# A ring of three score banks for the counts, inverses on 16 columns, and a joined pair of blocks in a decoder layer's attention

## The chip, the cores and the metric

The kernel runs on one core of a Trainium2 chip. The time is that of the device for one execution, in microseconds (us). The engines are TensorE (PE, with its weight loads as PEld), VectorE (DVE), ScalarE (ACT), GpSimd (POOL) and SyncE (SP), which only issues transfers here. All run their own instruction streams and wait for each other by semaphores.

## What is computed

A decoder layer in three parts, each on a layer norm of x and added to it: self-attention with two branches, cross-attention to a memory of 77 rows, and a feed-forward part with weights and activations rounded to FP4. The change touches the self-attention alone, cut to what matters (x is 2 x 2048 x 512, 16 heads of 32):

```python
decay_bias = -jnp.abs(pos[None, :] - pos[:, None]) * (1.0 - decay_factor)
out_short = _attention(q, k_s, v_s, decay_bias)   # softmax(q k^T / sqrt(32) + bias) v
out_long = _attention(q, k_l, v_l, None)
alpha = jax.nn.sigmoid(mix_weight)
out = alpha * out_short + (1.0 - alpha) * out_long
```

## The kernel before, in words

The program has three stages: `project` (projections, to about 480 us), `attend` (to 3794 us), and `finish` (the rest). `attend` treats 32 pairs of batch and head, each with two branches. One branch of one head is a unit, so there are 64 units; a pass of the loop has four (two heads), and `w` is the unit's number in its pass. Even `w` are short branches with the decay, odd ones long branches.

For a unit the scores are made twice. As queries by keys (`scores_qk`, tile `pa`, four PSUM banks), a chunk of 128 queries by 512 keys in a matmul; VectorE takes the row maxima of two chunks at once (`max_pair`). That runs one to two units ahead. The negated maxima are turned, and SyncE writes them as a row of `q_operand` (`place_max`). Then as keys by queries (`scores_kq`, tile `pb`, two banks), with the maxima already subtracted; ScalarE takes the exponential of each chunk of 128 keys by 512 queries into `probs_T`, which has eight slots (`PBUF`) for the 16 blocks of 128 keys.

A unit has 16 steps, one per block. In step `i` TensorE multiplies block `i` with V (`times_v`: four float32 matmuls, each on 32 columns of the array, shown as eight rows), and then issues eight score matmuls: four of `scores_kq` for blocks `i + 1` and `i + 2`, four of `scores_qk` for a later unit. A matmul of `scores_kq` waits for the exponential two chunks before it. In even units a chunk on the diagonal is cut in pieces, with small `kink` matmuls.

The softmax's denominators are sums over all 16 blocks. GpSimd adds ten of the blocks (`BY_POOL`) to `probs_added`, an instruction of 128x2048 each, and issues a DMA for each of the six others (`BY_DMA`), which adds them to `probs_poured` (`pour`; the first one copies). The order of both is `POOL_ORDER`. Each has to wait: an addition for the last one, a transfer for the landing of the last one. ScalarE may write block `b + 8` to the slot of `b` only once V's product, and the addition or the transfer of `b`, are done. Then TensorE sums over the partitions by matmuls with `ones` (`count`, in steps 4 and 6 of the next unit), into a PSUM bank of their own, `pc`.

VectorE's other work in a unit: it copies `outputs_T` from PSUM (`take`, step 15), inverts the sums in four reciprocals of 128x128 (steps 7 to 10), weighs (`weigh`, step 11) and after an odd unit adds both branches (`mix`, step 12). SyncE stores the result, and loads the next operands.

The order on each engine is that in which the loops above write it; nothing schedules it.

## Time and profile before

| what | us |
|---|---|
| median of three runs | 4903.88 (4898.86 to 4909.8) |
| the profiled execution | 4901.64 |
| its span, first to last instruction | 4899.8 |
| TensorE busy | 4676.8 (95%) |
| VectorE busy | 3911.0 (80%) |
| GpSimd busy | 3278.3 (67%) |
| ScalarE busy | 2928.4 (60%) |

The shares are over all stages. A row of PE is one matmul or several alike merged; matmuls are pipelined, so a row is longer than the time to the next one's start, and the time from start to start tells what a matmul costs. In square brackets stands how long the engine was idle before a row, and what ended that.

### The profile page before, as it was taken

How to read it: one execution, taken by the hardware profiler on the slowest of the kernel's cores; microseconds unless marked ns; L12 is line 12 of the kernel's file. 1: busy time of each engine (PE TensorE's matmuls, PEld its weight loads, DVE VectorE, ACT ScalarE, POOL GpSimd, SP SyncE). 2: the span in 40 equal slices, each digit the busy share in tenths (PEclk: the TensorE clock that was granted, in tenths of full speed). 3: DMA queues.
4: the chain of work that ended last, by engine and by line, in shares of the span. 5: the costliest groups of instructions: out<-in, count | busy, mean ns of one | idle time of the engine just before them, and what ended most of it. 6: DMA issues, size and time to landing. Idle time of an engine off the chain costs nothing. (4 is left out here: it accounts for less than half of the span.)

```text
span 4899.8 us, 94453 instructions
## 1 busy us (share of the span) xinstructions
PE 4676.8 (95%) x30732; PEld 2051.3 (42%) x30732; DVE 3911.0 (80%) x4625; ACT 2928.4 (60%) x5106; POOL 3278.3 (67%) x1268
## 2 busy tenths in 40 slices
PE   8998999999999999999999999999998799999998
PEld 3444233333333333333333333333332577777776
DVE  7567888888888888888888888888884588888887
ACT  3222367676766766766666666766666355555554
POOL 0000399998989989888898989989897233333332
PEclk9999799999999999999999999999999799999999
DMA  5444366666676666666666676666765100000000
GB/s 171 126 140 129 84 154 154 152 151 160 146 156 151 157 157 146 159 144 157 153 146 159 144 158 155 157 154 146 165 135 118 59 27 27 20 27 27 27 23 12
DMA packets 216646, 592.18 MB, mean 121 GB/s; under 512 B 46259, under 2 KB 120115, under 8 KB 167157
## 3 DMA queue, kind: packets, MB, share of 16 engines
q0 software_dynamic: 55008, 400.58, 37.6%
q1 hardware_dynamic: 161135, 185.60, 12.8%
q8 instruction: 258, 4.23, 0.3%
q14 instruction: 207, 1.70, 0.1%
q10 hardware_dynamic: 38, 0.08, 0.0%
HBM read 123.56 MB, written 61.64 MB: 38 GB/s over the span
## 5 line engine op out<-in xcount | busy, mean ns | idle before, releaser
L852 ACT ACTIVATE probs_T<-scores_kq 128x512 f32<-128x512 f32 x4096 | 2247.2, 595 | 992.3 <-PE scores_kq L959 819.4
L868 DVE TENSOR_REDUCE rowmax_parts<-scores_qk 128x1 f32<-128x1024 f32 x2048 | 2398.3, 1210 | 546.1 <-PE scores_qk L959 541.9
L804 POOL TENSOR_TENSOR probs_added<-probs_added,probs_T 128x2048 f32<-128x2048 f32 x510 | 2386.1, 4679 | 48.8 <-POOL probs_added L804 37.5
L959 PE MATMUL scores_kq<-q_operand,k_operand 103*128 103x512 f16 (+3 forms) x3712 | 1277.7, 350 | 77.9 <-ACT probs_T L852 69.0
L959 PE MATMUL scores_qk<-k_operand,q_operand 96*128 96x512 f16 (+4 forms) x3712 | 1125.0, 351 | 32.7 <-DVE rowmax_parts L868 17.0
L1025 PE MATMUL outputs_T<-probs_T,v_operand 128*32 128x512 f32 x8192 | 1095.7, 607 | 1.0 <-ACT probs_T L852 1.0
L959 PEld LDWEIGHTS scores_kq<-q_operand,k_operand 103*128 103x128 f16 x3712 | 358.5, 97 | 1072.6 <-ACT probs_T L852 842.0
L959 PEld LDWEIGHTS scores_qk<-k_operand,q_operand 96*128 96x128 f16 (+1 forms) x3712 | 362.4, 98 | 336.8 <-DVE rowmax_parts L868 101.7
L1647 PE MATMUL f_gate_up<-w_gate_up,xq_T 128*128 128x256 f16 (+1 forms) x4608 | 494.3, 266 | 7.7 <-DVE hidden L1538 6.5
L1647 PEld LDWEIGHTS f_gate_up<-w_gate_up,xq_T 128*128 128x128 f16 x4608 | 421.1, 98 | 77.0 <-issue 24.3
L816 POOL DMA_DIRECT2D probs_poured<-probs_T x318 | 275.8, 867 | 255.7 <-DMA probs_poured<-probs_T 186.9
L959 PE MATMUL scores_kq<-q_operand_above,k_operand 103*128 103x512 f16 (+3 forms) x1152 | 400.5, 348 | 1.9 <-ACT probs_T L852 1.5
L959 PE MATMUL scores_qk<-k_operand,q_operand_above 102*128 102x512 f16 (+3 forms) x1152 | 368.8, 351 | 0.0
L1355 POOL TENSOR_TENSOR hidden_parts<-hidden_q,hidden_parts 128x768 f16<-128x768 f32 x64 | 97.9, 1529 | 349.9 <-ACT hidden_parts L1430 349.9
L780 POOL MEMSET ones<- 128x32 f32 x1 | 0.1, 124 | 464.0 <-POOLq L216 464.0
L804 POOL TENSOR_TENSOR probs_added<-probs_T 128x2048 f32<-128x2048 f32 x64 | 296.9, 4639 | 14.6 <-ACT probs_T L852 14.6
L959 PEld LDWEIGHTS scores_kq<-q_operand_above,k_operand 103*128 103x128 f16 x1152 | 110.0, 96 | 434.0 <-ACT probs_T L852 424.8
L1025 PEld LDWEIGHTS outputs_T<-probs_T,v_operand 128*32 128x32 f32 x8192 | 161.8, 108 | 261.8 <-issue 251.7
L900 DVE RECIPROCAL sums<-sums 128x128 f32<-128x128 f32 x256 | 243.8, 954 | 25.7 <-PE sums L1032 25.7
L555 PE MATMUL products_p<-xn_T_parts,w_qkv_parts 128*128 128x512 f16 x1152 | 254.5, 381 | 2.9 <-DVE xn_T_parts L408 1.5
L1632 PE MATMUL f_down<-w_down,hidden_T 128*128 128x512 f16 x1056 | 245.3, 382 | 0.0
L555 PEld LDWEIGHTS products_p<-xn_T_parts,w_qkv_parts 128*128 128x128 f16 x1152 | 112.9, 98 | 136.5 <-issue 4.1
(166 smaller groups left out, 4113.9 us busy)
## 6 DMA issues: line engine op xcount, KB each, us to landing
probs_poured<-probs_T POOLq DMA_DIRECT2D x382, 1024.0 KB, 7.6
qk_parts_dram<-qk_parts SPq DMA_DIRECT2D x96, 256.0 KB, 2.9
q_operand<-qk_parts_dram SPq DMA_DIRECT2D x192, 128.0 KB, 3.4
k_operand<-qk_parts_dram SPq DMA_DIRECT2D x192, 128.0 KB, 4.0
v_dram<-v_heads SPq DMA_DIRECT2D x16, 1024.0 KB, 6.4
v_operand<-v_dram SPq DMA_DIRECT2D x64, 256.0 KB, 6.5
q_operand_above<-qk_parts_dram SPq DMA_DIRECT2D x96, 128.0 KB, 2.8
x_groups<-x SPq DMA_DIRECT2D x8, 1024.0 KB, 9.4
```

Source lines behind the costliest of these rows:

```text
L555: last = nc.tensor.matmul(mm[:, m % 4, :], w_parts[:, a, c, m * P:(m + 1) * P], xT[:, u, c, b, :], start=c == 0 and a == b, stop=c == KT - ...
L780: nc.gpsimd.memset(ones[:, :], 1.0).then_inc(consts, 1)
L804: nc.gpsimd.tensor_tensor(total, first, probs[:, b % PBUF, :], ALU.add).then_inc(added.sem, 1)
L816: nc.gpsimd.dma_start(total, probs[:, b % PBUF, :], accum_op=ALU.add).then_inc(landed.sem, 16)
L852: nc.scalar.activation(probs[:, kb % PBUF, qt * BANK:(qt + 1) * BANK], pb[:, k % 2, :], ACT.Exp)\
L868: nc.vector.reduce_max(rowmax[:, w % 2, g // 2, g % 2:g % 2 + 1], half, AX.X).then_inc(maxed.sem, 1)
L900: nc.vector.reciprocal(pc[:, r * P:(r + 1) * P], pc[:, r * P:(r + 1) * P]).then_inc(inverted.sem, 1)
L959: return nc.tensor.matmul(out, lhsT, rhs, start=start, stop=stop, skip_group_check=True)
L1025: last = nc.tensor.matmul(po[qt * HD:(qt + 1) * HD, :], v_op[:, w, kb, :], probs[:, kb % PBUF, qt * BANK:(qt + 1) * BANK], start=kb == 0, ...
L1355: nc.gpsimd.tensor_tensor(h16[:, 1, a:a + w], hq[:, a:a + w], h16[:, 0, a:a + w], ALU.subtract)\
L1632: last = nc.tensor.matmul(pd[:, :], hT[:, c, a, :], wd[:, c, b, :], start=opens and c == first and a == b, stop=ends and c == first + coun ...
L1647: last = nc.tensor.matmul(pg[:, k % 2, g, 0:w], xqT[:, n % 2, c, a, :], w_up[:, c, g, b, at:at + w], start=c == 0 and a == b, stop=c == KT ...
```

## The change

- `pb` has three banks, and `pc` is gone. Chunks of scores and the two counts of a unit take turns on the three banks: in the ring of 66 places of a unit, places 23 and 36 (`COUNT_SLOTS`) are the counts'. A matmul waits for the reader of the place three before it. TensorE issues one more chunk ahead (`LEAD = 3`), and two chunks of `scores_qk` stand side by side.
- The counts stand in steps 4 and 7; they no longer add up in one bank. ScalarE copies each to SBUF (`copy_sums`), SyncE packs four rows of 512 into 128x16 (`pack_sums`), VectorE adds both parts (`merge`) and takes a reciprocal of 16 columns at step 10 (`invert`), SyncE writes it to DRAM and reads it back spread over the partitions (`store_inverse`, `spread_inverse`).
- ScalarE takes `outputs_T` out of PSUM, times the branch's weight. GpSimd multiplies with the inverse and mixes (`weigh`), behind block 14 of the next unit.
- Block 0's exponential is written right to `probs_poured`. The transfers are those of blocks 1, 6, 9, 12 and 15. VectorE adds blocks 2 and 3 (`join`, ahead of the first pair of step 4), and GpSimd adds nine: 3 (joined), 4, 5, 7, 8, 10, 11, 13, 14.

```diff
-BY_DMA = (0, 3, 6, 9, 12, 15)
-BY_POOL = tuple(b for b in range(KB) if b not in BY_DMA)
+VISIT = 1
+LEAD = 3
+COUNTS_AT = (4, 7)
+BY_DMA = (1, 6, 9, 12, 15)
+JOINED = (2, 3)
+BY_POOL = (3, 4, 5, 7, 8, 10, 11, 13, 14)
...
+def emitted(i):
+    return (i + VISIT) * NQ + LEAD
+COUNT_SLOTS = (emitted(COUNTS_AT[0]), emitted(COUNTS_AT[1]) + 1)
+RING = CHUNKS + 2
+BANKS = 3
+def ring_of(c):
+    return c + sum(c + k >= slot for k, slot in enumerate(COUNT_SLOTS))
...
+        def block_of(w, kb):
+            return poured_sum[:, w % 2, :] if kb == 0 else probs[:, kb % PBUF, :]
...
+            def pack_sums(w, n, j):
+                wait_apart(sp, sums_out, sums_out.at(n, 2 * w + j + 1), passed)
+                wait_apart(sp, merged, merged.at(n, w), passed)
+                sp.dma_start(sums_c[:, j, :], sums[::HD, j, :]).then_inc(packed[j].sem, 16)
...
+            def weigh(w, n):
+                p, a = divmod(w, 2)
+                wait_apart(pool, taken, taken.at(n, w + 1), passed)
+                wait_apart(pool, inv_spread, inv_spread.at(n, w + 1), passed)
+                if a == 0:
+                    wait_apart(pool, stored[p], stored[p].before(n, NQ), passed)
+                    nc.gpsimd.tensor_tensor(o_mix[:, p, :], oT[:, 0, :], inv[:, 0, :], ALU.mult).then_inc(weighed.sem, 1)
+                    return
+                nc.gpsimd.tensor_tensor(oT[:, 1, :], oT[:, 1, :], inv[:, 1, :], ALU.mult).then_inc(weighed.sem, 1)
+                wait_apart(pool, weighed, weighed.at(n, w + 1), passed)
+                nc.gpsimd.tensor_tensor(o_mix[:, p, :], o_mix[:, p, :], oT[:, 1, :], ALU.add).then_inc(mixed.sem, 1)
...
+            def join(w, n):
+                a, b = JOINED
+                dve.wait_ge(expd.sem, expd.at(n, (w * KB + b + 1) * NQ))
+                dve.wait_ge(summed.sem, summed.at(n, w * KB + b + 1))
+                nc.vector.tensor_tensor(block_of(w, b), block_of(w, a), block_of(w, b), ALU.add).then_inc(joined.sem, 1)
...
+            def invert(w, n, total):
+                dve.wait_ge(inv_stored.sem, inv_stored.at(n, w))
+                nc.vector.reciprocal(inv_c[:, :], total).then_inc(inverted.sem, 1)
...
+            def bank_free(w, n, r):
+                r -= BANKS
+                if r < 0:
+                    w, r = w - 1, r + RING
+                if r in COUNT_SLOTS:
+                    pe.wait_ge(sums_out.sem, sums_out.at(n, 2 * (w - 1) + COUNT_SLOTS.index(r) + 1))
+                else:
+                    c = r - sum(r > slot for slot in COUNT_SLOTS)
+                    pe.wait_ge(expd.sem, expd.at(n, w * CHUNKS + c + 1))
```

On GpSimd a unit before, in the order of the program, from the issue for block 12 of one unit to that of the next (L804 is an addition, L816 and L813 are issues; the semaphores it waits for are in brackets, `x2` is two alike):

```order
L816 DMA probs_poured<-probs_T 128x2048 [waits a_exp,a_poured1]
L804 TENSOR_TENSOR probs_added<-probs_added,probs_T 128x2048 [waits a_exp,a_added]
L816 DMA probs_poured<-probs_T 128x2048 [waits a_exp,a_poured1]
L813 DMA probs_poured<-probs_T 128x2048 [waits a_exp,a_counted_poured]
L804 TENSOR_TENSOR probs_added<-probs_T 128x2048 [waits a_exp,a_counted]
L804 TENSOR_TENSOR probs_added<-probs_added,probs_T 128x2048 [waits a_exp,a_added]
L816 DMA probs_poured<-probs_T 128x2048 [waits a_exp,a_poured0]
L804 TENSOR_TENSOR probs_added<-probs_added,probs_T 128x2048 [waits a_exp,a_added] x2
L816 DMA probs_poured<-probs_T 128x2048 [waits a_exp,a_poured0]
L804 TENSOR_TENSOR probs_added<-probs_added,probs_T 128x2048 [waits a_exp,a_added] x2
```

Now, from the same block's issue (L892) on, with `weigh` of an odd unit (L879, L881) between:

```order
L892 DMA probs_poured<-probs_T 128x2048 [waits a_exp,a_poured0]
L868 TENSOR_TENSOR probs_added<-probs_added,probs_T 128x2048 [waits a_exp,a_added] x2
L879 TENSOR_TENSOR o_T<-o_T,sums_inverse 128x512 [waits a_o_taken,a_inverse_spread]
L881 TENSOR_TENSOR o_mixed<-o_mixed,o_T 128x512 [waits a_weighed]
L892 DMA probs_poured<-probs_T 128x2048 [waits a_exp,a_poured0]
L892 DMA probs_poured<-probs_T 128x2048 [waits a_exp,a_pv]
L868 TENSOR_TENSOR probs_added<-probs_T 128x2048 [waits a_exp,a_joined,a_counted0]
L868 TENSOR_TENSOR probs_added<-probs_added,probs_T 128x2048 [waits a_exp,a_added]
```

Between the issues for block 12 and block 15 stood one addition, and two stand there now with the weighing. The first addition of a unit waits for the join.

On VectorE a unit's middle before (L868 is a pair of maxima, L900 a reciprocal, L910 the weighing, L895 the take):

```order
L868 TENSOR_REDUCE rowmax_parts<-scores_qk 128x1 [waits a_scored_qk] x16
L900 RECIPROCAL sums<-sums 128x128 [waits a_counted_poured]
L868 TENSOR_REDUCE rowmax_parts<-scores_qk 128x1 [waits a_scored_qk] x2
L900 RECIPROCAL sums<-sums 128x128 [waits a_counted_poured]
L868 TENSOR_REDUCE rowmax_parts<-scores_qk 128x1 [waits a_scored_qk] x2
L900 RECIPROCAL sums<-sums 128x128 [waits a_counted_poured]
```

And now (L983 is the pair, L1012 the join, L1018 the merge, L1024 the reciprocal):

```order
L983 TENSOR_REDUCE rowmax_parts<-scores_qk 128x1 [waits a_scored_qk] x19
L1012 TENSOR_TENSOR probs_T<-probs_T 128x2048 [waits a_pv,a_exp]
L983 TENSOR_REDUCE rowmax_parts<-scores_qk 128x1 [waits a_scored_qk] x12
L987 TENSOR_REDUCE negmax<-rowmax_parts 128x16 [waits a_maxed]
L1018 TENSOR_REDUCE sums_merged<-sums_compact 128x16 [waits a_sums_packed1,a_sums_packed0]
L983 TENSOR_REDUCE rowmax_parts<-scores_qk 128x1 [waits a_scored_qk]
L1024 RECIPROCAL sums_inverse_compact<-sums_merged 128x16 [waits a_inverse_stored,a_sums_merged]
```

One long instruction stands ahead of step 4's pairs, and the short ones are gathered at step 10.

## Rows read from the trace of the kernel before

**Rows 1.** The page: the span, and each engine's busy time.

```profile
span 4899.8 us, 94453 instructions
PE 4676.8 (95%) x30732; PEld 2051.3 (42%) x30732; DVE 3911.0 (80%) x4625; ACT 2928.4 (60%) x5106; POOL 3278.3 (67%) x1268
```

**Rows 2.** Lines, 1200 to 3600 us: busy us, mean ns, idle before.

```profile
L1025 PE MATMUL outputs_T<-probs_T,v_operand 128*32 128x512 f32 x6070 | 811.5, 606 | 0.1
```

**Rows 3.** Timeline of PE, a quiet step: start us, us, instruction.

```profile
1613.05 1.07 PE L1025 MATMUL outputs_T<-probs_T,v_operand 128*32 128x512 f32 x8
1615.65 0.38 PE L959 MATMUL scores_kq<-q_operand,k_operand 103*128 103x512 f16 x1
...
1615.96 0.64 PE L1025 MATMUL outputs_T<-probs_T,v_operand 128*32 128x512 f32 x4
```

**Rows 4.** Timeline of PE, first rows of units 40, 41, 51 and 52.

```profile
2573.64 0.64 PE L1025 MATMUL outputs_T<-probs_T,v_operand 128*32 128x512 f32 x4
...
2623.32 1.06 PE L1025 MATMUL outputs_T<-probs_T,v_operand 128*32 128x512 f32 x8
...
3128.16 1.07 PE L1025 MATMUL outputs_T<-probs_T,v_operand 128*32 128x512 f32 x8
...
3177.24 1.06 PE L1025 MATMUL outputs_T<-probs_T,v_operand 128*32 128x512 f32 x8
```

**Rows 5.** Timeline, 1608 to 1661 us, one unit's handover of slots.

```profile
1608.23 0.84 POOL L816 DMA_DIRECT2D probs_poured<-probs_T  x1
...
1618.14 3.37 ACT L852 ACTIVATE probs_T<-scores_kq 128x512 f32<-128x512 f32 x6 [2.58 <-DMA probs_poured<-probs_T]
...
1619.36 0.87 POOL L816 DMA_DIRECT2D probs_poured<-probs_T  x1 [5.72 <-issue]
...
1620.71 4.66 POOL L804 TENSOR_TENSOR probs_added<-probs_T 128x2048 f32<-128x2048 f32 x1
1620.76 0.16 PEld L1025 LDWEIGHTS outputs_T<-probs_T,v_operand 128*32 128x32 f32 x8 [0.30 <-issue]
...
1623.70 2.35 DVE L868 TENSOR_REDUCE rowmax_parts<-scores_qk 128x1 f32<-128x1024 f32 x2 [1.41 <-PE scores_qk L959]
...
1660.32 0.88 POOL L816 DMA_DIRECT2D probs_poured<-probs_T  x1
```

**Rows 6.** The tile `probs_poured`, 1200 to 3600 us: issue to landing.

```profile
DMA to landing us min/median/max: 6.9/7.6/10.7
```

**Rows 7.** Waits, 1200 to 3600 us: us in total, times, longest.

```profile
ACT probs_T L852 <- DMA probs_poured<-probs_T: 94.7, 65, 3.4
...
PE scores_qk L959 <- DVE rowmax_parts L868: 8.7, 24, 0.4
...
PE scores_kq L959 <- DMA q_operand_above<-negmax_T: 2.5, 2, 1.6
```

**Rows 8.** Timeline of PE, step 11 of the same unit.

```profile
1642.95 1.06 PE L1025 MATMUL outputs_T<-probs_T,v_operand 128*32 128x512 f32 x8
...
1646.33 0.64 PE L1025 MATMUL outputs_T<-probs_T,v_operand 128*32 128x512 f32 x4
```

**Rows 9.** Lines by form, whole run: prices of like operations elsewhere.

```profile
L401 DVE SCALAR_TENSOR_TENSOR w_qkv_parts<-w_qkv,w_qkv_parts 128x2048 f16<-128x2048 f32 x5 | 11.2, 2284 | 1.1 <-ACT w_qkv_parts L512 1.1
...
L1345 POOL TENSOR_TENSOR x_quantised<-x_quantised,x_exponents 128x512 f32<-128x512 f32 x32 | 40.7, 1271 | 2.5
```

**Rows 10.** Small transfers (KB, us to landing), and the timeline behind the last counts.

```profile
q_operand<-negmax_T SPq DMA_DIRECT2D x188, 1.0 KB, 2.2
...
3785.27 3.40 DVE L900 RECIPROCAL sums<-sums 128x128 f32<-128x128 f32 x4 [4.46 <-PE sums L1032]
...
3789.57 0.69 DVE L918 TENSOR_TENSOR o_mixed<-o_weighed,sums 128x512 f32<-128x512 f32 x1
```

**Rows 11.** Timeline of the last stage: a VectorE operation just behind a GpSimd one.

```profile
4309.60 1.64 POOL L1355 TENSOR_TENSOR hidden_parts<-hidden_q,hidden_parts 128x768 f16<-128x768 f32 x1 [10.70 <-ACT hidden_parts L1430]
4309.66 2.26 DVE L113 TENSOR_TENSOR hidden_q<-hidden_q,f_scale 128x640 f32<-128x640 f32 x1
```

More of the change, by code:

```diff
@@ L756, in one_pass @@
                 for w in range(UNITS):
+                    back = unit_before(w, n, first)
+                    if back:
+                        for j in range(2):
+                            pack_sums(*back, j)
+                        store_inverse(*back)
                     if after(w, n, last):
                         place_max(*after(w, n, last))
-                    if w == 0 and not first:
+                    if back:
+                        spread_inverse(*back)
+                    if w == 1 and not first:
                         store(1, n - 1)
-                    if w == 2:
+                    if w == 3:
                         store(0, n)
@@ L778, in _ @@
         def _(pool):
-            give_credit(pool, [maxed, expd, summed, added, counted, taken, weighed, counted_poured] + stored)
+            give_credit(pool, [maxed, expd, summed, joined, added, sums_out, merged, inv_stored, inv_spread, taken, weighed]
+                        + counted + packed + stored)
             nc.gpsimd.memset(ones[:, :], 1.0).then_inc(consts, 1)
@@ L798, in add @@
                 if b == BY_POOL[1]:
[L799 to L800 removed]
+                    first = block_of(w, BY_POOL[0])
+                    wait_apart(pool, joined, joined.at(n, w + 1), passed)
+                    wait_apart(pool, counted[0], counted[0].at(n, w - 1), passed)
                 else:
@@ L826, in one_pass @@
                             add(w, n, b)
+                        if b == WEIGH_BEHIND and unit_before(w, n, first):
+                            weigh(*unit_before(w, n, first))
             one_pass(0, True, False)
@@ L832, in _ @@
             one_pass(PASSES - 1, False, True)
+            weigh(UNITS - 1, PASSES - 1)
         @block.scalar
@@ L836, in _, with block_free @@
             load_positions(act, 0)
+            def block_free(w, n, kb, first):
+                if kb == 0:
+                    act.wait_ge(counted[1].sem, counted[1].at(n, w - 1))
+                    return
+                u, b = (w, kb - PBUF) if kb > PBUF else (w - 1, kb + PBUF) if kb < PBUF else (w - 1, kb)
+                act.wait_ge(summed.sem, summed.at(n, u * KB + b + 1))
+                if b == JOINED[0]:
+                    act.wait_ge(joined.sem, joined.at(n, u + 1))
+                elif b in BY_POOL:
+                    act.wait_ge(added.sem, added.at(n, u * ADDS + adds_until(b)))
+                elif u >= 0 or not first:
+                    landed = poured[u % 2]
+                    act.wait_ge(landed.sem, landed.at(n, u // 2 * POURS + BY_DMA.index(b) + 1))
@@ new lines, in copy_sums, with take @@
+            def copy_sums(w, n, j):
+                act.wait_ge(counted[j].sem, counted[j].at(n, w + 1))
+                act.wait_ge(packed[j].sem, packed[j].at(n, w))
+                nc.scalar.copy(sums[:, j, :], pb[:, COUNT_SLOTS[j] % BANKS, :]).then_inc(sums_out.sem, 1)
+            def take(w, n):
+                act.wait_ge(summed.sem, summed.at(n, (w + 1) * KB))
+                if w % 2 == 0:
+                    act.wait_ge(weighed.sem, weighed.at(n, w - 1))
+                elif w == 3:
+                    act.wait_ge(mixed.sem, mixed.at(n, 1))
+                elif not isinstance(n, int) or n > 0:
+                    act.wait_ge(mixed.sem, mixed.before(n, 2))
+                nc.scalar.activation(oT[:, w % 2, :], po[:, :], ACT.Copy, scale=gates[:, 3 + w % 2:4 + w % 2])\
+                    .then_inc(taken.sem, 1)
@@ L859, in _ @@
             one_pass(PASSES - 1, False, True)
+            take(UNITS - 1, PASSES - 1)
+            act.wait_ge(counted[0].sem, counted[0].at(PASSES - 1, UNITS))
+            act.wait_ge(packed[0].sem, packed[0].at(PASSES - 1, UNITS - 1))
+            nc.scalar.copy(sums[:, 0, :], pb[:, RING % BANKS, :]).then_inc(sums_out.sem, 1)
         @block.vector
@@ L923, in one_pass @@
                     for i in range(KB):
-                        if i == KB - 1:
-                            take(w, n)
-                        if back and INVERT <= i < INVERT + NQ:
-                            invert(*back, i - INVERT)
-                        if back and i == WEIGH:
-                            weigh(*back)
                         distance, chunks = chunks_of(i)
                         unit = after(w, n, last, distance)
+                        if back and i == INVERT:
+                            merge(*back)
+                        if i == JOIN:
+                            join(w, n)
                         for c in chunks[::2] if unit else ():
@@ L947, in _ @@
             one_pass(PASSES - 1, False, True)
-            for r in range(NQ):
-                invert(UNITS - 1, PASSES - 1, r)
-            weigh(UNITS - 1, PASSES - 1)
-            mix(1, PASSES - 1)
+            dve.wait_ge(packed[0].sem, packed[0].at(PASSES - 1, UNITS))
+            invert(UNITS - 1, PASSES - 1, sums_c[:, 0, :])
         @block.tensor
```

216 lines of the change are left out of this document (108 added, 108 removed).

## The prediction, made blind

> **What bounds the kernel now.** The page comes first. TensorE is busy for 95% of 4899.8 us, and VectorE comes next with 80% [rows 1]. TensorE alone can't say what the attention stage costs, because a busy matmul row can hide a wait before it. So the second view is the list of lines for 1200 to 3600 us: 6070 rows of `outputs_T`, 128 to a unit (16 steps of 8), are 47.4 units in 2400 us, which makes 50.6 us a unit [rows 2]. The third is the timeline of PE, read from the start of one `outputs_T` group to the next, since each step opens with one.
>
> A quiet step in an odd unit runs from 1613.05 to 1615.96, 2.91 us, for the four products with V and eight score matmuls [rows 3]. A whole quiet even unit takes 49.68 us (2573.64 to 2623.32), a quiet odd one 49.08 us (3128.16 to 3177.24) [rows 4], so 49.4 in the mean. The real mean is 1.2 us above that. With 64 units, 77 us of the stage is waiting, and all the rest is TensorE's own work.
>
> Where the 1.2 us lie is seen in step 3 of the unit that starts at 1607.24: it lasts from 1615.96 to 1620.76, 4.80 us in place of 2.91 [rows 3, 5]. ScalarE stood 2.58 us until 1618.14 for a DMA into `probs_poured` [rows 5]: block 4 wants the slot that block 12 of the last unit held. That transfer was issued only at 1608.23, behind the addition of block 13, and takes 7.6 us to land, 10.7 at most [rows 5, 6]. GpSimd then waits for the same landing before it can issue the next transfer (1619.36, after 5.72 us idle), and starts its additions over at 1620.71 [rows 5]. Its round from one transfer of block 12 to the next is 1608.23 to 1660.32, 52.1 us, of which 39.6 are a solid run of eight additions and three issues (1620.71 to 1660.32). So two rings of nearly one length turn against each other: TensorE's 49.4 and GpSimd's 46.4 plus its wait. In the list of waits, ScalarE's for this DMA are 94.7 us in 65 pieces over 47.4 units [rows 7]. Part of that is idle time that it has anyway.
>
> VectorE is the smaller part. Where the reciprocals and the weighing stand, TensorE's second pair of `scores_qk` banks comes free late. Step 11 of the same unit runs from 1642.95 to 1646.33, 3.38 us in place of 2.91 [rows 8]. The list of waits has 24 such waits, one to each odd unit, of 8.7 us in all, so 0.36 each [rows 7].
>
> **The change part by part.**
>
> GpSimd's round. It loses the plain copy of block 0 (ScalarE writes it to the sum itself) and one addition (blocks 2 and 3 come joined), and gets `weigh`. From the join on it again has eight additions and three issues, 39.6 us by the same run of rows. Then weigh: 1.27 us [rows 9], twice for an odd unit with the mix, so 1.3 or 2.8 with the gaps, then two issues at about 0.65. Its own work is 42.2 to 43.7 us of a unit of 49.4. It no longer waits for a transfer with nothing between: block 12's goes out after six additions and two issues, about 29.6 us behind the join, and 10 us of additions follow before block 15's.
>
> When does the join stand? VectorE ends the second pair of step 3 about 1.3 us into step 4, which is 4 x 2.91 + 1.3 = 13.0 us into the unit. The join is one `TENSOR_TENSOR` of 128x2048 with both inputs in SBUF. The nearest row is 2.28 us, 128x2048 on VectorE while GpSimd idles [rows 9]. So the additions start at 15.4 us and end at 55.0.
>
> Are the slots in time? Block 12's transfer goes out at 45.0 and lands at 52.6 (55.7 at worst). With three scores ahead block 4's first score is the fourth matmul of step 2, at 1.65, and ScalarE wants the slot 0.4 us later, 0.84 before step 3 begins. Step 3 of the next unit begins at 49.3 + 8.7, so that is 57.2 us after the unit's start: 1.5 to 4.6 us to spare. Block 15's goes out at 56.3 to 57.8 and lands at 63.9 to 65.4 (68.5 at worst). Block 7 is wanted 0.84 before step 6, at about 67.0. That is the tightest, 1.6 to 3.1 us to spare at the median, and short only in a rare odd unit. All others have over 4 us. I leave 0.1 us a unit for it, and 0.2 for single hold-ups of another cause, as the two of TensorE for the row of maxima, 2.5 us [rows 7]. So 0.9 of the 1.2 us go.
>
> VectorE's stalls. Four reciprocals, a copy, a weighing and half a mix leave it. The 0.47 us of step 11 go in odd units; even units, whose pieces are longer, and step 10 lose about 0.1 each. That is (0.47 + 0.1 + 0.12) / 2 = 0.35 us a unit; from below it is the 8.7 us of waits over 47.4 units, 0.18 [rows 7]. The new reciprocal has an eighth of the columns of one that took 0.85 us (3.40 for four [rows 10]).
>
> The join's own price. Steps 4 and 5 have room: in the trace VectorE sits idle 1.41 us before the first pair of step 4 (1623.70), as the count stands there [rows 5]. Two reductions take 2.36. In the new order the pair is written by two neighbouring matmuls. Join from 1.35 to 3.64 us of step 4, pairs until 4.82 and 6.00. Step 5 begins at 3.77. Its first pair wants its banks at 4.99, and they are free; its second at 5.85, and gets them at about 6.1. So 0.25 us a unit stay. From below it is nothing (kinked steps of even units are 0.1 longer); from above, with no idle time to lie in, 2.28 less the usual 0.55 a step, about 1.2 us.
>
> ScalarE gets three copies per unit at about 0.56 each (six exponentials in 3.37 us [rows 5]). It has 64 of these in 49.4 us, so 36 of 49.4 become 38: no cost. The copy of the sums (ready 1.95 us into the step, done 2.55) frees its ring slot just before score 25 wants it at 2.73. The take stands at step 15 between two scores. The third bank gives at most that: quiet steps have no wait on ScalarE to remove, since after the last score 0.31 us pass before the next `outputs_T` group in every step [rows 3].
>
> SyncE's added queue entries (two packs, a store and a spread per unit) stand in steps 4 to 12. The row of negated maxima now waits behind the store of the inverse, one issue, and has three steps until it is read. No cost.
>
> The tail. After the last unit nothing hides the new chain: copy 0.6, pack 2.2, reciprocal 0.3, store 2.2, spread 3.3 (2.2 us is the row of a small transfer [rows 10]; the spread has 256 KB, for which I add 1.1), weigh and mix 2.8, so 11.4 us in place of the reciprocals, weighing and mix, which end 5.0 us after the counts (3785.27 to 3790.26 [rows 10]). That is 6 to 7 us more, all on the path, as the next stage starts when the store has landed.
>
> The sum: 50.6 - 0.9 - 0.35 + 0.25 = 49.6 us a unit, 1.0 less. Over 62 steady units 62 us, less 7 of the tail: 55. The profiled execution took 4901.6 us beside a median of 4903.9, so 4847 for a profiled run and **4849 us** for the median. If the join costs nothing and slot waits go wholly, 16 + 6 more go (4827); if the join costs 1.2 us, 59 come back (4908); if 0.4 of the waits stay, 19 (4868).
>
> What the Trainium skill says, weighed here: a VectorE and a GpSimd instruction can shut each other out. The row first: a VectorE product of 128x640 that began at 4309.66, 0.06 us after a GpSimd operation of 1.64 us, took 2.26 us [rows 11], which is the rest of that operation and its own time. "SBUF — State Buffer", section "Who interferes with whom", says the same as a rule: a VectorE instruction with two SBUF inputs and a GpSimd one that reads SBUF exclude each other for the whole instruction. The trace agrees. The join is of that kind, so what it costs hangs on GpSimd being idle at 13.0 us.
>
> **Rivals.**
>
> *The join meets an addition.* A join that starts while GpSimd adds waits for what is left of 4.66 us [rows 5], 2.3 in the mean, with VectorE's pairs and so TensorE behind it. For it: rows 11. Against: GpSimd is done with the last unit at 8.2 to 9.7 us (55.0 + 2.6 or 4.1 - 49.4) and can't add before the join, as its first addition waits for it. The point from which it decides is a run of 39.6 that becomes 43, or a 12th block's transfer that lands over 5 us late. Price: 49.6 + 2.3 = 51.9 us a unit, 1.3 x 62 = 81 more than before, with the tail 4990 us, slower.
>
> *The slot wait only moves.* Block 7 then waits for block 15's transfer as block 4 did for 12's. For it: landings up to 10.7 us [rows 6], and two issues in a row now (15 and the next unit's 1). Against: the spare time above. If the whole 0.9 stays, 50.5 us a unit, -6 + 7: 4905 us, no change.
>
> *It hides wholly.* All waits of both kinds go and the join fits into the count: 49.4 - 0.35 = 49.05 a unit, 96 less, plus 7: 4815 us. Against: single long steps have other causes than slots.
>
> **How the numbers follow.** Forecast 0.60 (its own range 4825 to 4882), the join meets an addition 0.13, the wait moves 0.13, hides wholly 0.14. A difference of 0.2%, 10 us, is about what a measurement can tell from none. Faster: nearly all of the forecast's 0.60, hides wholly 0.14, so 0.73. Same: 0.09 of the moved wait and a bit of the forecast's end, 0.10. Slower: 0.13 of the join and 0.04 of a moved wait that costs more, 0.17. The range 4808 to 4910 takes in the forecast's bounds one by one, most of the moved wait and half of the case below, and leaves out the join that meets an addition: 0.8.
>
> **What would show it.** Gaps between `outputs_T` groups: steps 3 and 0 back to 2.9 to 3.0 us, step 11 of odd units at 2.91, step 5 longer by 0.1 to 0.4. GpSimd idle 3 to 5 us before each `joined` addition, and the join at 2.3 us throughout; 4 us and more there means the first rival. ScalarE's waits for `probs_poured` near zero; if they stand at block 7, the second. From the end of the last counts to the end of the last mix 11 to 12 us in place of 5.0. The forecast fails if quiet steps themselves change length, since I take TensorE's own time as untouched.

## The result, and the profile after

| | median us | range | runs |
|---|---|---|---|
| before | 4905.1 | 4898.86 to 4909.8 | 4 |
| after | 4790.0 | 4789.02 to 4790.97 | 4 |

The ratio is 0.9769, with a 95% interval of 0.9757 to 0.978: 115 us faster, where 55 were forecast. The time lies 18 us below the range. The profiled execution took 4789.35 us. The page of after, as [rows 1] of before:

```profile
span 4787.3 us, 95755 instructions
PE 4623.8 (97%) x30732; PEld 2081.9 (43%) x30732; DVE 3784.0 (79%) x4400; ACT 2984.2 (62%) x5297; POOL 3069.2 (64%) x1236
```

The list of lines for 1200 to 3600 us of after, which answers to [rows 2]. Block 0 now has a row of its own, as it is read from `probs_poured`:

```profile
L1143 PE MATMUL outputs_T<-probs_T,v_operand 128*32 128x512 f32 x5916 | 789.0, 605 | 0.3 <-issue 0.3
...
L1143 PE MATMUL outputs_T<-probs_poured,v_operand 128*32 128x512 f32 x392 | 52.2, 605 | 0.3 <-issue 0.3
```

5916 + 392 rows at 128 a unit are 49.3 units in 2400 us, 48.7 us each. From the first `outputs_T` group to that of the last unit, by start times, a unit takes 50.52 us before and 48.70 after: 1.82 x 63 = 115 us. The chain behind the last unit costs 9.8 us more, and the last stage is 5.8 us shorter in this profile, though its code is the same. Over the fourteen profiles of this document it takes 1095.7 to 1108.8 us, and longer where TensorE stood longer at half the clock (1.2 GHz): 62 us of it in the two shortest, 90 and 92 in the two longest, 88 in before and 73 in after. So medians that differ by less than some 13 us are read from the unit times too.

The list of waits of after for 1200 to 3500 us (us in total, times, longest), beside [rows 7]:

```profile
PEld scores_qk L1066 <- DVE rowmax_parts L983: 7.5, 24, 0.3
...
PE scores_kq L1066 <- DMA q_operand_above<-negmax_T: 3.7, 5, 0.9
...
POOL probs_poured L892 <- DMA probs_poured<-probs_T: 1.8, 3, 0.7
...
ACT probs_T L961 <- DMA probs_poured<-probs_T: 1.5, 5, 0.4
```

ScalarE's 94.7 us for the poured transfers are 1.5 now, so in these units the slot ring has stopped holding anything up. The wait of matmuls for the row of maxima grew, from 2.5 to 3.7 us. The first line has its like not in [rows 7] but in this one of before (1200 to 3600 us); the 8.7 us of PE itself in [rows 7] have no line any more:

```profile
PEld scores_qk L959 <- DVE rowmax_parts L868: 63.3, 142, 0.9
```

In the last unit, which computes no maxima, the steps are 2.40 us and TensorE is quicker than GpSimd's round. There a slot wait is back, at block 7, whose slot block 15's transfer held. The timelines of ACT and PE in its step 6, which starts at 3633.38 and takes 7.59 us:

```profile
3638.31 3.53 ACT L961 ACTIVATE probs_T<-scores_kq 128x512 f32<-128x512 f32 x7 [5.31 <-DMA probs_poured<-probs_T]
```

```profile
3638.96 2.08 PE L1066 MATMUL scores_kq<-q_operand,k_operand 103*128 103x512 f16 x4 [4.52 <-ACT probs_T L961]
```

Behind it stands after's only stretch at half the clock between the stage's first step and its last, 6.8 us from 3638.1 on.

The timeline of PE of after, the starts of steps 3, 4, 5 and 6 of a quiet odd unit, as [rows 3]:

```profile
2848.46 1.06 PE L1143 MATMUL outputs_T<-probs_T,v_operand 128*32 128x512 f32 x8
...
2851.36 1.06 PE L1143 MATMUL outputs_T<-probs_T,v_operand 128*32 128x512 f32 x8
...
2855.11 1.07 PE L1143 MATMUL outputs_T<-probs_T,v_operand 128*32 128x512 f32 x8
...
2858.01 1.06 PE L1143 MATMUL outputs_T<-probs_T,v_operand 128*32 128x512 f32 x8
```

Step 3 takes 2.90 us where [rows 5] had 4.80, step 4 with its count 3.75, and step 5, behind the join, 2.90. The prediction had 3.15 for that one. The medians over units 4 to 59, of the steps that changed most, say where else something changed:

| step | 0 | 2 | 3 | 5 | 6 | 7 | 10 | 11 | 12 |
|---|---|---|---|---|---|---|---|---|---|
| even, before | 3.22 | 3.00 | 3.05 | 3.00 | 3.74 | 3.00 | 3.02 | 3.13 | 3.03 |
| even, after | 2.96 | 2.95 | 2.96 | 2.95 | 2.95 | 3.81 | 2.90 | 3.02 | 3.02 |
| odd, before | 2.91 | 2.91 | 4.23 | 2.90 | 3.76 | 2.91 | 3.01 | 3.38 | 2.92 |
| odd, after | 2.90 | 2.90 | 2.90 | 2.90 | 2.90 | 3.76 | 2.84 | 2.84 | 2.84 |

Besides steps 0, 3 and 11, many steps that the prediction took as fixed are 0.04 to 0.12 us shorter.

The timelines of VectorE and GpSimd of after, around the join of that unit:

```profile
2850.32 2.35 DVE L983 TENSOR_REDUCE rowmax_parts<-scores_qk 128x1 f32<-128x1024 f32 x2 [0.54 <-PE scores_qk L1066]
2852.59 2.28 DVE L1012 TENSOR_TENSOR probs_T<-probs_T 128x2048 f32<-128x2048 f32 x1
2854.78 4.61 DVE L983 TENSOR_REDUCE rowmax_parts<-scores_qk 128x1 f32<-128x1024 f32 x4
```

```profile
2848.29 1.76 POOL L892 DMA_DIRECT2D probs_poured<-probs_T  x2
2855.15 4.53 POOL L868 TENSOR_TENSOR probs_added<-probs_T 128x2048 f32<-128x2048 f32 x1 [5.10 <-ACT probs_T L961]
```

GpSimd issues its transfers 8.5 us into the unit and idles 5.1 us; the join stands at 12.8 to 15.1 and the first addition at 15.4. All of these are where the prediction put them.

The timeline behind the last counts of after, and of before the store and the next stage's first issue, which stand behind [rows 10]:

```profile
3668.88 0.58 ACT L974 COPY sums<-scores_kq 128x512 f32<-128x512 f32 x1 [4.46 <-PE scores_kq L1150]
3669.61 0.55 SPq L773 DMA_DIRECT2D sums_compact<-sums  x1
3671.49 0.25 DVE L1024 RECIPROCAL sums_inverse_compact<-sums_compact 128x16 f32<-128x16 f32 x1 [19.87 <-DMA sums_compact<-sums]
3671.90 0.34 SPq L779 DMA_DIRECT2D sums_inverse_dram<-sums_inverse_compact  x1
3673.48 0.55 SPq L787 DMA_DIRECT2D sums_inverse<-sums_inverse_dram  x1
3678.34 1.26 POOL L879 TENSOR_TENSOR o_T<-o_T,sums_inverse 128x512 f32<-128x512 f32 x1 [12.67 <-DMA sums_inverse<-sums_inverse_dram]
3679.78 1.26 POOL L881 TENSOR_TENSOR o_mixed<-o_mixed,o_T 128x512 f32<-128x512 f32 x1 [0.18 <-POOL o_T L879]
3681.14 1.72 SPq L794 DMA_DIRECT2D attention_dram<-o_mixed  x4
3687.15 0.43 SPq L1388 DMA_DIRECT2D wo_sb<-L_attn_Wo  x1
```

```profile
3790.28 1.72 SPq L742 DMA_DIRECT2D attention_dram<-o_mixed  x4
3793.80 0.42 SPq L1284 DMA_DIRECT2D wo_sb<-L_attn_Wo  x1
```

The chain takes 12.2 us from the copy to the end of the mix, and its store 6.0 where it took 3.5; no run shows why the store is longer.

### The profile page after: what moved, and what is told of

Read it like the earlier page. It is cut to its first block and busy times, and to the rows that moved or that the text cites. A ratio compares the mean times of both kernels' runs of the same rounds, so it can differ in the third digit from the quotient of the medians.

```text
span 4787.3 us, 95755 instructions
## 1 busy us (share of the span) xinstructions
PE 4623.8 (97%) x30732; PEld 2081.9 (43%) x30732; DVE 3784.0 (79%) x4400; ACT 2984.2 (62%) x5297; POOL 3069.2 (64%) x1236
## 3 DMA queue, kind: packets, MB, share of 16 engines
q1 hardware_dynamic: 195563, 203.94, 15.1%
q8 instruction: 258, 4.23, 0.4%
## 5 line engine op out<-in xcount | busy, mean ns | idle before, releaser
L983 DVE TENSOR_REDUCE rowmax_parts<-scores_qk 128x1 f32<-128x1024 f32 x2048 | 2411.4, 1218 | 549.3 <-PE scores_qk L1066 547.7
L961 ACT ACTIVATE probs_T<-scores_kq 128x512 f32<-128x512 f32 x3840 | 2072.9, 600 | 622.7 <-PE scores_kq L1066 562.1
L868 POOL TENSOR_TENSOR probs_added<-probs_added,probs_T 128x2048 f32<-128x2048 f32 x446 | 2077.1, 4657 | 47.8 <-POOL probs_added L868 44.9
L1066 PE MATMUL scores_kq<-q_operand,k_operand 103*128 103x512 f16 (+3 forms) x3712 | 1175.9, 349 | 20.2 <-DMA q_operand_above<-negmax_T 10.4
L1143 PE MATMUL outputs_T<-probs_T,v_operand 128*32 128x512 f32 x7680 | 1024.7, 605 | 1.0 <-ACT probs_T L961 0.7
L1066 PE MATMUL scores_qk<-k_operand,q_operand 96*128 96x512 f16 (+4 forms) x3712 | 985.7, 349 | 22.4 <-DMA v_operand<-v_dram 14.6
L868 POOL TENSOR_TENSOR probs_added<-probs_T 128x2048 f32<-128x2048 f32 x64 | 290.7, 4543 | 349.2 <-ACT probs_T L961 349.2
L1066 PE MATMUL scores_kq<-q_operand_above,k_operand 103*128 103x512 f16 (+3 forms) x1152 | 339.6, 344 | 1.0 <-ACT probs_T L961 1.0
L1066 PE MATMUL scores_qk<-k_operand,q_operand_above 102*128 102x512 f16 (+3 forms) x1152 | 329.7, 349 | 0.0
L892 POOL DMA_DIRECT2D probs_poured<-probs_T x318 | 276.3, 912 | 76.5 <-ACT probs_T L961 69.4
L1143 PEld LDWEIGHTS outputs_T<-probs_T,v_operand 128*32 128x32 f32 x7680 | 151.2, 108 | 355.9 <-ACT probs_T L961 310.0
L936 ACT COPY sums<-scores_kq 128x512 f32<-128x512 f32 x126 | 73.8, 585 | 159.6 <-PE scores_kq L1150 159.6
```

What stands on the lines that cost most here:

```text
L868: nc.gpsimd.tensor_tensor(total, first, block_of(w, b), ALU.add).then_inc(added.sem, 1)
L892: nc.gpsimd.dma_start(total, block_of(w, b), accum_op=ALU.add).then_inc(landed.sem, 16)
L936: nc.scalar.copy(sums[:, j, :], pb[:, COUNT_SLOTS[j] % BANKS, :]).then_inc(sums_out.sem, 1)
L961: nc.scalar.activation(block_of(w, kb)[:, qt * BANK:(qt + 1) * BANK], pb[:, ring_of(c) % BANKS, :], ACT.Exp).then_inc(expd.sem, 1)
L983: nc.vector.reduce_max(rowmax[:, w % 2, g // 2, g % 2:g % 2 + 1], half, AX.X).then_inc(maxed.sem, 1)
L1066: return nc.tensor.matmul(out, lhsT, rhs, start=start, stop=stop, skip_group_check=True)
```

## The experiments

The unit times below are means over the 63 starts, in each kernel's own profile. A ratio is against before, measured in the same job, with its 95% interval.

**Before with its two waits taken away.** The first kernel pours a quarter of the columns, the second inverts 16 columns of each 128, the third does both.

```diff
-nc.gpsimd.dma_start(total, probs[:, b % PBUF, :], accum_op=ALU.add)
+nc.gpsimd.dma_start(total[:, 0:BANK], probs[:, b % PBUF, 0:BANK], accum_op=ALU.add)
```

> The kernel before, but each transfer that adds a block to the poured sum moves 512 of the 2048 columns (the denominators lack the rest), so a slot held by a transfer comes free some 4 to 5 us sooner. Theory A (slot waits were 1.20 us of each unit, the excess of 50.52 over the quiet 49.32): the gaps of steps 0 and 3 fall to 2.9 to 3.0 and the time to 4905 - 76 = 4829, within 4820 to 4840. Theory B, the prediction's own size (0.9 us a unit could go): 4849. Rival C (the wait only moves to another slot or engine): 4895 to 4905.

```diff
-nc.vector.reciprocal(pc[:, r * P:(r + 1) * P], pc[:, r * P:(r + 1) * P])
+nc.vector.reciprocal(pc[:, r * P:r * P + 16], pc[:, r * P:r * P + 16])
```

> The kernel before, but each of the four reciprocals of a unit takes 16 of its 128 columns (the other columns stay uninverted). Theory A: steps 9 to 12 of odd units and 11 of even ones lose 0.40 us a unit in the mean, but while the GpSimd round stays as long part of it comes back as slot wait, so between 4880 and 4900. If the two waits simply add: 4905 - 25 = 4880. If VectorE did not matter: 4905.

> The kernel before with both edits, thin transfers and thin reciprocals. Theory A: 4905 - 76 - 25 = 4804, and 14 us more than the changed kernel's 4790, since the third bank (0.36 us a unit, 23 us) is missing and the longer tail (10 us) too. Theory D (the third bank is worth nothing, as the prediction said, and its order neither): the quiet steps of even units are 2.95 here too, and the time is 4780 or less, as the tail is the short one.

| | median us | ratio | unit |
|---|---|---|---|
| thin pours | 4816.1 | 0.9822 (0.9806 to 0.9839) | 49.30 |
| thin reciprocals | 4899.8 | 0.9995 (0.9985 to 1.0004) | 50.65 |
| both | 4790.9 | 0.9775 (0.9758 to 0.9791) | 48.91 |

The slot waits were worth 1.22 us a unit, all that I had counted. The expected 4829 was 13 us too high, of which the last stage, 10.3 us shorter in this profile, makes 10. Both thin parts came 13 us under the expected 4804 too, with 8.0 of it in the last stage. Even steps stand at 3.00 there, so the sign that Theory D named isn't there. Thin reciprocals alone are worth nothing that can be measured, but 25 us once the pours are thin. The waits of the kernel with thin reciprocals alone (1200 to 3600 us) show why:

```profile
POOL probs_poured L816 <- DMA probs_poured<-probs_T: 152.2, 49, 5.1
ACT probs_T L852 <- DMA probs_poured<-probs_T: 106.9, 65, 3.5
```

GpSimd's round sets the unit there: it waits for its own transfers as long as in before (152.2 us, 150.6 before), and for ScalarE only 20.7 (19.3 before). What VectorE gives back, ScalarE waits away: 106.9 us in place of 94.7 [rows 7]. A part goes to TensorE's clock. This trace has 13 stretches at half of it between the stage's first step and its last, of 3.4 or 6.8 us, each in or behind a long step, where before's has four. Half of their sum, 27 us here and 7 there, is the most that they can cost. The two shares weren't separated.

**After with the old order of chunks, with three banks and with two.** The first puts a chunk of `scores_kq` and one of `scores_qk` in turn, as before; the second also lets each place wait for the one two before it.

```diff
-for half in range(2):
-    scores(at)
-    maxima(step, 2 * half)
-    scores(at + 1)
-    at += 2
+scores(at)
+maxima(step, 0)
+scores(at + 1)
+maxima(step, 1)
+maxima(step, 2)
+scores(at + 2)
+maxima(step, 3)
+scores(at + 3)
```

(`maxima` issues one chunk per call in place of two.)

> The changed kernel with the score matmuls of a step in the order of before (kq, qk, kq, qk, qk, kq, qk, kq), three banks kept. Theory A1 (the third bank alone removes the small waits in each step): quiet steps stay at 2.95 and 2.84, time 4785 to 4797. Theory A2 (it is the order with two qk side by side that does it): even steps go back to 3.00, and +20 us or more, 4810.

```diff
 def bank_free(w, n, r):
-    r -= BANKS
+    r -= 2
```

> The changed kernel with the order of before inside a step, and each score matmul waiting for the reader of the place two before it instead of three, so that the third bank gives no slack. Theory A1 (the third bank's slack is worth 0.36 us a unit): even steps at 3.00, odd steps from 2.84 to 2.89, time 4790 + 23 = 4813, within 4805 to 4830. Theory D (the bank gives nothing): 4790 within 5.

Old order: 4825.6 us, ratio 0.9837 (0.9821 to 0.9854), unit 49.21. Two deep as well: 4880.6, 0.996 (0.9946 to 0.9975), unit 50.07. The second came out slower than either theory said. The first fits Theory A2's time (20 us or more), but not its sign: quiet even steps stay at 2.96, as Theory A1 said. With the old order, all steps stay within 0.02 us of after's but step 5, whose medians are 3.26 (even) and 3.32 (odd) in place of 2.95 and 2.90. The timelines of VectorE and PE in that step of an odd unit, which starts at 2878.59:

```profile
2876.27 2.28 DVE L1012 TENSOR_TENSOR probs_T<-probs_T 128x2048 f32<-128x2048 f32 x1
2878.47 4.61 DVE L983 TENSOR_REDUCE rowmax_parts<-scores_qk 128x1 f32<-128x1024 f32 x4
```

```profile
2880.87 0.39 PE L1066 MATMUL scores_qk<-k_operand,q_operand 102*128 102x384 f16 x2 [0.24 <-DVE rowmax_parts L983]
```

The second pair's banks come free late, at 2.28 us into the step, and TensorE stands. That is the join's price with this order, 0.3 to 0.4 us.

With two banks, the steps with a count are 0.34 longer (4.16 and 4.10 for 3.82 and 3.77), and step 15, with the take, 0.26 (even) and 0.29 (odd). Step 5, behind the longer count, is back at 2.96 and 2.98. The timelines of ACT and PE in such a step, which starts at 2915.95:

```profile
2917.94 0.58 ACT L936 COPY sums<-scores_kq 128x512 f32<-128x512 f32 x1 [1.24 <-PE scores_kq L1150]
```

```profile
2918.58 0.39 PE L1066 MATMUL scores_kq<-q_operand,k_operand 103*128 103x512 f16 x1 [0.17 <-ACT sums L936]
```

A count that passes through the ring holds up the second score behind it until ScalarE has copied it. Besides, even steps 6, 8 and 9 stand at 3.00 in place of 2.96, and odd steps 10 to 13 at 2.88 in place of 2.84, as in the kernel with both thin parts. Even steps 2 and 3, at 3.00 and 3.01 in that one, stay at 2.96 with two banks. Where no maxima are computed, in the last six steps of unit 62 and in unit 63, a step takes some 0.49 longer: a plain one 2.88 in place of 2.40. The third bank so does three things. It hides what the change itself puts into the ring, it takes 0.04 off seven steps of each pair of units, and 0.49 off those without maxima. The timelines of ACT and PE of before show a wait of 0.04, in step 2 of an even unit (it ends at 2582.56). This is one of the steps that two banks don't bring back; the wait is of the same kind, but it wasn't the third bank that took it away:

```profile
2580.98 1.08 ACT L852 ACTIVATE probs_T<-scores_kq 128x512 f32<-128x512 f32 x2 [0.67 <-PE scores_kq L959]
```

```profile
2581.87 0.38 PE L959 MATMUL scores_qk<-k_operand,q_operand 96*128 96x512 f16 x1
2582.12 0.23 PE L959 MATMUL scores_kq<-q_operand,k_operand 103*128 103x128 f16 x1
```

The score starts 0.25 us after the row before it, where others follow at 0.22, and 0.06 after the exponential's end. No idle time is printed, so only starts show it.

**After, two deep, its own order.** Only the edit of `bank_free`.

> The changed kernel in its own order, waiting two places back. Two kq matmuls stand side by side, so the third waits for an exponential that ends at 2.02 us of the step where it could start at 1.88, and the last for one that ends at 2.67 where it could start at 2.53: 0.2 to 0.3 us a step in 1000 steps. Theory A: 4990 to 5090. Theory D: 4790.

5047.2 us, ratio 1.0297 (1.028 to 1.0314), unit 52.66. Two chunks of `scores_qk` side by side also put two of `scores_kq` side by side, and these need the third bank: without it the new order costs 257 us more than after.

**The join's price.** The join on 16 columns, alone and with the old order.

```diff
-nc.vector.tensor_tensor(block_of(w, b), block_of(w, a), block_of(w, b), ALU.add)
+nc.vector.tensor_tensor(block_of(w, b)[:, 0:16], block_of(w, a)[:, 0:16], block_of(w, b)[:, 0:16], ALU.add)
```

> The changed kernel, the join on 16 of 2048 columns (block 2 is missing from the denominators elsewhere). From the trace the join costs TensorE nothing, since its second pair is free 0.07 us before it is wanted: 4790 within 5. The prediction's size (0.25 us a unit) would give 4774.

> The changed kernel with the matmul order of before inside a step and the join on 16 columns. In the run with the old order alone step 5 was 0.30 us longer in even units and 0.42 in odd ones. If that is the join's price, which the new order hides: step 5 is back at 2.96 and 2.91, and 4826 - 23 = 4803 or a little less. If the order has that price by itself: 4826.

| | median us | ratio | unit |
|---|---|---|---|
| new order, thin join | 4775.7 | 0.9748 (0.9732 to 0.9764) | 48.55 |
| old order, thin join | 4793.1 | 0.977 (0.9754 to 0.9786) | 48.73 |

With the old order the thin join gives 32 us back, and step 5 falls to 2.96 and 2.90: there the price is real. With the new one every step's median stays as it was. The 14 us that it gave all the same, against the 0 expected, are single long steps (the mean of odd step 14 goes from 3.18 to 3.01, 7 us over the stage, and one long step each in units 60 and 61 gives 2) and 6 us in the last unit (44.7 to 38.5). There step 6 falls from 7.59 to 3.22, and ScalarE's wait for the slot from 5.3 to 1.1. GpSimd's additions start behind the join, so they and block 15's transfer can be earlier without it. So the join has no price on the path that the prediction gave it, but a price by what comes behind it.

**An extra VectorE sum where GpSimd adds, and where it doesn't.** It tests the first rival's mechanism. A sum of 128x128 in SBUF stands at step 3 and at step 8.

```diff
+EXTRA_AT = (3, 8)
...
+if i in EXTRA_AT:
+    dve.wait_ge(spared.sem, spared.at(n, 2 * w + EXTRA_AT.index(i)))
+    nc.vector.tensor_tensor(spare[:, :], ident[:, :], ident[:, :], ALU.add).then_inc(spared.sem, 1)
```

> The changed kernel with two added VectorE sums of 128x128 in each unit, both inputs in SBUF: one ahead of step 3's pairs, where GpSimd does not add, and one ahead of step 8's, in the middle of GpSimd's run of additions. Exclusion theory (the first rival's mechanism): the one at step 3 takes 0.2 to 0.3 us; the one at step 8 starts about 1.4 us into an addition in every unit and lasts till its end, 3 to 3.5 us, VectorE's pairs come late and TensorE loses 2 to 2.5 us a unit: 4790 + 140 = 4930. Theory without exclusion: both take 0.3 us, 4790 to 4795.

4995.7 us, ratio 1.0185 (1.0167 to 1.0203), unit 52.11. Its timelines of VectorE and GpSimd:

```profile
2917.41 0.28 DVE L1042 TENSOR_TENSOR spare<-ident_f 128x128 f32<-128x128 f32 x1
...
2933.63 4.08 DVE L1042 TENSOR_TENSOR spare<-ident_f 128x128 f32<-128x128 f32 x1
```

```profile
2932.74 4.81 POOL L871 TENSOR_TENSOR probs_added<-probs_added,probs_T 128x2048 f32<-128x2048 f32 x1
```

At step 3 GpSimd is idle and the sum takes 0.28 us. At step 8 it begins 0.89 us into an addition, and ends 0.16 after it: 4.08 us for the same work. Over all units the medians are 0.28 at step 3 and 3.95 at step 8. Step 3 keeps its length, step 9 goes from 2.90 to 5.55 (odd, median). The rival is a true mechanism, and the join in after escapes it by its place. The cost of 206 us is over the expected 140. "SBUF — State Buffer" of the Trainium skill, section "Who interferes with whom", has a VectorE instruction with two SBUF inputs and a GpSimd one that reads SBUF shut each other out. The trace agrees, 0.28 us against 4.08.

Part of the cost is TensorE's clock: the trace has 29 stretches at half the clock between the stage's first step and its last, of 3.4 or 6.8 us, where after's has the one in its last unit. They are 147 us together, so they can cost half of that at most. No run separates this share of the 206 us from the rest. The windows view of 600 to 3600 us gives the granted clock third from the end, for after and (all engines) for this kernel:

```profile
600.00:3600.00 3000.00, 2992.24 (x19696) 1.00 0.68 142
```

```profile
600.00:3600.00 3000.00, 2873.43 (x18384) 987.43 (x18383) 2541.61 (x2242) 2077.12 (x3853) 2425.28 (x832) 0.98 0.64 134
```

**The row of maxima behind the transfers.** After's odd units sometimes have a long step 14. In the timelines of PE and SP of after, for the worst one:

```profile
2592.14 0.23 PE L1066 MATMUL scores_kq<-q_operand,k_operand 103*128 103x128 f16 x1 [0.92 <-DMA q_operand_above<-negmax_T]
```

```profile
2582.02 3.50 SPq L767 DMA_DIRECT2D q_operand<-negmax_T  x4
2585.57 3.93 SPq L767 DMA_DIRECT2D q_operand_above<-negmax_T  x4
```

Eight small transfers take SyncE 7.5 us to issue, and the last lands as the unit needs it. Three kernels look for the cause. One makes after's pours a quarter as wide (the edit of thin pours). One issues the row ahead of the inverse's store, and shortens the last unit's chain: VectorE inverts, weighs and mixes there straight from PSUM, as before. The third is that, and ScalarE issues four of the eight transfers between exponentials.

```diff
-        store_inverse(*back)
     if after(w, n, last):
         place_max(*after(w, n, last))
     if back:
+        store_inverse(*back)
         spread_inverse(*back)
...
-dve.wait_ge(packed[0].sem, packed[0].at(PASSES - 1, UNITS))
-invert(UNITS - 1, PASSES - 1, sums_c[:, 0, :])
+dve.wait_ge(counted[0].sem, counted[0].at(m, UNITS))
+nc.vector.reciprocal(total, total).then_inc(inverted.sem, 1)
...
+PLACED_AT = (49, 51, 53, 55)
+if w % 2 and ahead and c in PLACED_AT:
+    place_part(*ahead, PLACED_AT.index(c))
```

> The changed kernel, each transfer of a block moving 512 of its 2048 columns (the denominators lack the rest). If slots are never waited for any more, steps 0 to 13 stay as they are. If the hold-ups of step 14 are the row of maxima landing behind these transfers, they vanish in odd units (0.23 us each in the mean) and in units 60 and 61: 4790 - 10 = 4780. If not: 4790.

> The changed kernel with two edits: SyncE writes the row of maxima ahead of the store of the inverse, and the last unit's sums are inverted and weighed by VectorE straight from the PSUM bank as before. The tail from the last count to the last mix falls from 12.2 to 5 us (-7), and the hold-ups of step 14, 9 us in all, halve (-4): 4779. If the hold-ups come from the transfers being slow to land and not from their place in the queue, 4783. If neither matters: 4790.

> The version with the short tail, and the four transfers of the row of maxima for the second query operand issued by ScalarE in steps 10 to 13 instead of behind the first four by SyncE. If the hold-ups of step 14 come from eight issues in a row of 0.5 to 1 us on one queue, they go (9 us in all): 4775. If they come from landings that are slow behind the large transfers, they stay: 4784.

| | median us | ratio | mean odd step 14 |
|---|---|---|---|
| thin pours | 4781.5 | 0.9747 (0.9731 to 0.9763) | 2.95 |
| short tail | 4784.1 | 0.9762 (0.9746 to 0.9778) | 3.14 |
| rows by ScalarE too | 4779.3 | 0.9747 (0.9731 to 0.9763) | 3.03 |

The time to landing of `negmax_T` (1200 to 3600 us, min, median and max) in before, in after, and with thin pours:

```profile
DMA to landing us min/median/max: 1.6/1.9/7.1
```

```profile
DMA to landing us min/median/max: 1.6/4.5/6.5
```

```profile
DMA to landing us min/median/max: 1.6/2.0/3.6
```

So the pours delay the row, not the store ahead of it: with the store moved nearly all of the hold-ups stayed. In after the row's transfers go out 2.3 us (median) behind the issue of a poured one, in before 6.4. With half the issues on ScalarE over half of the hold-ups went (after has 3.18), but a step of 8.05 us stands in unit 60, and the unit is 48.70 us as in after. The short tail takes its 9.8 us (its store goes out 5.0 us after the counts' end, and the stage's tail is 14.7 as before), but gave 6 in the median; its unit is 48.72. The last kernel has the lowest median of those that compute the whole reference, 11 us below after. In the profiles 7 of it lie between the start of the last unit and the next stage, 4 in the last stage, and none in the 63 units. Its interval overlaps after's (0.9757 to 0.978) and those of the two beside it.

## Why the prediction was wrong

The direction, the places and the schedule were right; three terms of the sum were not. In us per unit, with what the runs gave:

| term | predicted | measured | from |
|---|---|---|---|
| slot waits | -0.9 | -1.22 | 50.52 to 49.30, thin pours on before |
| late rows of maxima | in the 0.3 left | +0.16 | 48.54 to 48.70, thin pours on after |
| VectorE's reciprocals | -0.35 | -0.39 | 49.30 to 48.91 |
| quiet steps | 0 | -0.37 | 48.91 to 48.54, both thin parts on before to thin pours on after |
| join, at step 5 | +0.25 | 0 | no step's median moves without it |
| sum | -1.0 | -1.82 | 50.52 to 48.70 |

- **"I leave 0.1 us a unit for it, and 0.2 for single hold-ups."** Nearly all slot waits went, block 7's too (ScalarE's 1.5 us in 2300), up to unit 60, though the transfers land later than forecast (8.4 us at the median and 13.1 at most, for 7.6 and 10.7). The hold-ups that came are another kind, and are about as large as the 0.2. The thin join takes 0.15 of them too, so they need the join as well as wide pours. Net 1.06 in place of 0.9, so 10 us. Thin pours on before also move fewer bytes, and before's trace has four stretches of 3.4 us at half the clock in this stage (at 1922, 2165, 3342 and 3660 us), each in or behind a long step, and the kernel with thin pours none; so up to 0.11 of the 1.22 can be the clock's.
- **VectorE's stalls.** Right in size. What the prediction did not see is that they pay only with the slot waits gone, which the thin reciprocals alone showed. Its first step, "77 us of the stage is waiting, and all the rest is TensorE's own work", was wrong here: the quiet units of 49.68 and 49.08 us that it took as TensorE's own hold these stalls and the 0.37 below.
- **"The third bank gives at most that: quiet steps have no wait on ScalarE to remove."** This step failed, by 0.37 x 63 = 23 us, the largest piece. I looked at one quiet step of an odd unit [rows 3], where it holds. In many even steps and in odd steps 10 to 13 there was 0.04 to 0.05 to gain. The third bank's part follows from the two-bank kernel, whose steps show it again: three steps of an even unit and four of an odd one, 9 of the 23 us. Some 2.6 more stand in unit 62, whose steps without maxima fall from 2.88 to 2.40. The 0.05 of even steps 2 to 5 (6 us) and the 0.12 of even step 10 (4 us) are not the bank's, as they are gone with two banks also. The kernels in which they are gone share, among others, one chunk more ahead (`LEAD`), the counts in the ring and less work on VectorE; no run takes these apart, so that cause stays open. The rest is 0.01 or less a step.
- **"Its second at 5.85, and gets them at about 6.1. So 0.25 us a unit stay."** The price of a late second pair was real, but it belongs to the old order (0.30 and 0.42 at step 5, as the old order with and without the join shows). In the new one the pairs end in the trace at 4.65 and 5.78 us of step 4, not 4.82 and 6.00: step 3's last pair is written earlier, and the join starts at 1.23 us of step 4 (2852.59), where with the old order it starts at 1.45 (2876.27 in a step from 2874.82). The banks are wanted at 5.85, so 0.07 us are to spare. That is 16 us of the miss. Some of it is luck: the thin join shows about as much, 14 us, paid behind the join, in single long steps and in the last unit, which the sum didn't have.
- **The tail.** 9.8 us for 7: the copy-to-mix chain is 12.2 us (11.4 forecast), and the final store lands 2.5 later. No row stood behind the 1.1 us that the forecast added for the spread; from its issue (3673.48) to GpSimd's weighing (3678.34) it took 4.9 us, for 3.3. The last unit's own length came out as before, 44.7 us, by two things that the forecast lacked: steps of 2.40 for 2.88, and the slot wait of step 6.
- **The first rival** did not happen, and the extra sums show that its condition, GpSimd adding at that moment, decides it. **The second** did not up to unit 60 (1.5 us), but block 7 did wait in the last unit, 5.3 us. **The third** came nearest: its 4815 had both kinds of waits wholly gone and the join free. What it lacks to 4790 is the quiet steps' 23 us. "The forecast fails if quiet steps themselves change length" was written, and they did.

The pieces (10 + 3 + 23 + 16, less 3 of the tail, and the last stage's 6) make 55 of the 60 us between forecast and result. Counting 62 units for 63 makes 1 more, and the stage's first step, 1.6 us earlier in after, 1.6.

## What to carry to other kernels

When a ring of banks gets one slot more, measure the steps in which the ring's reader is last, not one quiet step: a start 0.04 us late, which no view prints as idle, was some 9 us in 220 steps here. Two rings of nearly one length hide each other's stalls, so their gains don't add: one alone was worth nothing here, and 25 us behind the other. Look at the last units by themselves, as their steps are shorter and a ring that had time to spare elsewhere can hold them up. An accumulation that passed through a ring of two cost 0.34 us, and nothing that shows with three; and the order of the chunks and the depth belong together: the order alone was worth 35 us with three banks and -167 with two.

## What the runs showed of the hardware

- A VectorE sum of 128x128 with both inputs in SBUF took 0.28 us with GpSimd idle and 4.08 inside a GpSimd addition of 4.81; over the 64 units its median was 0.28 at the first place and 3.95 at the second.
- Small transfers of SyncE landed in 4.5 us at the median when they were issued 2.3 us behind GpSimd's large ones, in 2.0 when those were a quarter as wide, and in 1.9 in before, where they are issued 6.4 us behind.
- With the extra sums TensorE fell to half the clock (1.2 GHz) in 29 stretches. After has one, behind the long wait in its last unit, and its two-bank form none, though its units are longer still (52.66 us). There the time is lost in every step (3.11 to 3.17 for 2.90 to 2.96, medians), with the extra sums in one (step 9, 5.29 and 5.55), so the length of the unit alone does not decide it.
- The last stage, with the same code, took 1095.7 to 1108.8 us over fourteen kernels. TensorE stood at half the clock in it for 62 us in the two shortest, and for 90 and 92 us in the two longest.
